# Time mix of a Perceiver block on one Trainium2 core: exponents from one difference, projections by feature chunk, gate product before the division

## Chip, cores and metric

The kernel runs on one core of one Trainium2 chip. The metric is device time in microseconds of one execution of the whole program, as the median of several runs. The kernel before takes 1672.26 us in the median of 3 runs (1671.02 to 1672.91).

## The reference, cut to the part concerned

The program is a two-layer Perceiver-like model on 8 sequences of 64 tokens with 512 features, all in float32: windowed attention, full attention, a quantised feed-forward layer, cross attention over 1601 context tokens, then an RWKV block (time mix and channel mix), and a small last layer. The change is inside the RWKV block's time mix. `time_first`, `time_decay` and the mixes are vectors over the 512 features.

```python
xa = _ln(x, ln1_g, ln1_b)
xx = _shift(xa)                       # one token back, zero before the first
xk = xa * time_mix_k + xx * (1 - time_mix_k)      # the same for xv, xr
k = xk @ att_Wk.T;  v = xv @ att_Wv.T;  r = xr @ att_Wr.T
w = -jnp.exp(time_decay)
def step(carry, kv_t):
    aa, bb, pp = carry
    kk, vv = kv_t
    ww = time_first + kk
    p = jnp.maximum(pp, ww)
    e1 = jnp.exp(pp - p)
    e2 = jnp.exp(ww - p)
    out = (e1 * aa + e2 * vv) / (e1 * bb + e2)
    ww2 = pp + w
    p2 = jnp.maximum(ww2, kk)
    e1b = jnp.exp(ww2 - p2)
    e2b = jnp.exp(kk - p2)
    return ((e1b * aa + e2b * vv, e1b * bb + e2b, p2), out)
rwkv = jax.nn.sigmoid(r) * out_of_all_steps
x = x + rwkv @ att_Wo.T
```

## The kernel before, in words

**Layout.** 512 tokens are 4 tiles of 128 (NT = 4), 512 features are 4 chunks of 128 (KC = 4). The time mix works with features on partitions: each chunk is a tile of 128 partitions by 512 tokens (8 sequences of 64), or by 520 where each sequence has one padding column for the past (`padded`). Everything is in SBUF; the weights `awk`, `awv`, `awr`, `awo` are loaded long before. PSUM has 8 banks of 128x512.

**Order.** There is no scheduler: each engine's instruction list is written out in its block function and runs in that order, and semaphores tie the lists together. In `time_mix`:

- PE turns the normalised input (`Turned.tensor`, L1487), ScalarE takes it out with gain and shift (L1493), GpSimd forms the difference to the past token (L1501), VectorE makes the mixes xk, xv, xr, a chunk at a time (L1508).
- PE then does the projections k, v and r (L1545 to L1553), each with all four chunks of its mix at hand, bank by bank: the outer loop goes over output chunks o, the inner one (in `linear_to_features`, L136) over input chunks c. k goes to banks 4 to 7, v to 0 to 3, r to 4 to 7. ScalarE copies k to `kp` (L1568), a chunk as soon as its bank is done.
- `exponents(o)` on VectorE: the running maximum `top` by a scan (L1620), the output's maximum `p_now` (L1626), the exponents of the present token in the output (p2, L1628) and of the past in the state (p3, L1629). GpSimd makes the other two, p1 (L1588) and p4 (L1589). `p_now` is double buffered, so VectorE waits for GpSimd two chunks behind.
- ScalarE takes the exponential of the four tiles in place (L1573), then copies v's chunk (L1575); after all four chunks it makes the sigmoid of r (L1578).
- GpSimd multiplies by v (L1594, L1595), for all four chunks; VectorE's `sums(o)` (L1635 to L1643) does the scans for denominator and numerator, products, sums, the reciprocal (L1641) and the product with it (L1643). GpSimd multiplies the result by the gate (L1599), queued behind its eight products.
- PE does the output projection when all four chunks of `gate` are ready (L1555), token tile by token tile (L128 in `linear_to_tokens`). VectorE adds each tile to the residual (L1651) and normalises it for the next block (L91, L92, L97), with two small GpSimd instructions in between (L110, L112).

The next block, `channel_mix`, starts when all of this is done, and only then issues the transfer of its second weight.

## Time and profile before

| | |
|---|---|
| median of 3 runs | 1672.26 us (1671.02 to 1672.91) |
| the profiled execution | 1670.92 us |
| its span in the trace | 1669.1 us |
| mean granted TensorE clock | 0.916 |
| busy in the span: PE, VectorE, ScalarE, GpSimd | 1452.6, 775.1, 466.5, 558.5 us |
| the time mix, from the first mix on VectorE to the last normalised tile | 1406.8 to 1504.6 us |

The span is the time from the first to the last instruction of the profiled execution; 1.8 us of that execution lie around it. Engines are PE (TensorE's matmuls), PEld (its weight loads), DVE (VectorE), ACT (ScalarE), POOL (GpSimd) and SP. A float32 matmul appears as two records, so a projection of 16 matmuls has 32. `<-` behind a bracketed number names what ended the idle time before the instruction. The shares of busy time over the whole span describe mostly the cross attention; for the time mix one has to read its own 98 us.

### The profile page before, as it was taken

The numbers are of one execution on the slowest core, as the hardware profiler recorded it, in microseconds if no ns is written. First come the engines' busy times: TensorE is split into PE (matmuls) and PEld (weight loads), VectorE is DVE, ScalarE is ACT, GpSimd is POOL, SyncE is SP. The second block draws the span as 40 slices with busy tenths as digits, with TensorE's granted clock in tenths as the row PEclk, the third lists the DMA queues.
The fourth block names the chain that finished last, engine by engine and source line by source line (L and its number), as shares of the span: only waits on it lengthen the run. The fifth ranks groups of instructions, "written<-read, shape, count | busy, mean of one in ns | idle before, by whom it ended". The sixth has DMA issues, their size and how long they took to land. (4 is left out here: it accounts for less than half of the span.)

```text
span 1669.1 us, 26535 instructions
## 1 busy us (share of the span) xinstructions
PE 1452.6 (87%) x11120; PEld 1061.9 (64%) x11120; DVE 775.1 (46%) x1333; ACT 466.5 (28%) x772; POOL 558.5 (33%) x315
## 2 busy tenths in 40 slices
PE   7778976567998999999999999999998896836796
PEld 3556765233544778888788888888886673315573
DVE  2454279989525342332323323222332316978913
ACT  0323201031112214243243433324243431303302
POOL 6101057656324043132122223132143224617701
PEclk9778965788998999999999999999999997967997
DMA  5300030010101411011011111111012116003000
GB/s 236 151 1 1 0 139 1 0 70 0 76 0 57 151 56 57 30 53 54 31 53 52 45 43 47 42 45 57 31 61 62 44 38 255 0 0 120 1 0 26
DMA packets 50101, 91.29 MB, mean 55 GB/s; under 512 B 28600, under 2 KB 41664, under 8 KB 46912
## 3 DMA queue, kind: packets, MB, share of 16 engines
q1 hardware_dynamic: 49984, 89.60, 15.2%
q8 instruction: 90, 1.47, 0.4%
q14 instruction: 27, 0.22, 0.0%
HBM read 79.89 MB, written 9.70 MB: 54 GB/s over the span
## 5 line engine op out<-in xcount | busy, mean ns | idle before, releaser
L1082 POOL TENSOR_TENSOR ctx_hi<-ctx_raw,one 128x1536 fp32r<-128x1536 f32 (+1 forms) x36 | 103.0, 2860 | 598.7 <-DMA ctx_raw<-in_ctx 369.6
L1367 DVE TENSOR_SCALAR_CACHE_REDUCE E<-PS 128x384 f32<-128x384 f32 (+1 forms) x256 | 131.8, 571 | 177.1 <-PE PS L1155 176.6
L1264 ACT COPY ET<-PS 128x512 f32<-128x512 f32 (+1 forms) x224 | 129.8, 586 | 292.5 <-PE PS L1178 223.5
L1336 DVE TENSOR_TENSOR V<-PS,vbias 128x512 f32<-128x512 f32 (+1 forms) x104 | 71.8, 691 | 218.4 <-PE PS L1122 218.3
L1178 PE MATMUL PS<-ident,E 128*128 128x128 f32 (+1 forms) x832 | 124.7, 275 | 8.9 <-ACT ET L1264 8.8
L1085 POOL TENSOR_TENSOR ctx_raw_r<-ctx_raw,ctx_hi 128x1536 fp32r<-128x1536 f32 (+1 forms) x36 | 131.3, 3647 | 2.8
L1122 PE MATMUL PS<-wv_lo,ctx_hi 128*128 128x512 f32 (+1 forms) x416 | 128.0, 408 | 0.0
L1122 PE MATMUL PS<-ctx_raw_r,wk_hi 128*128 128x384 f32 (+1 forms) x512 | 127.3, 354 | 0.0
L1122 PE MATMUL PS<-ctx_hi,wk_hi 128*128 128x384 f32 (+1 forms) x512 | 120.7, 357 | 2.3 <-POOL ctx_raw_r L1085 2.3
L1271 ACT ACTIVATE E<-E,peak 128x1601 f32<-128x1601 f32 x64 | 103.5, 1623 | 68.1 <-DVE peak L1372 68.1
L1122 PE MATMUL PS<-wv_hi,ctx_hi 128*128 128x512 f32 (+1 forms) x416 | 120.6, 412 | 0.8 <-issue 0.8
L1178 PEld LDWEIGHTS PS<-ident,E 128*128 128x128 f32 (+1 forms) x832 | 99.8, 140 | 28.6 <-ACT ET L1264 11.9
L1122 PE MATMUL PS<-ctx_hi,wk_lo 128*128 128x384 f32 (+1 forms) x512 | 113.8, 344 | 0.0
L1122 PE MATMUL PS<-wv_hi,ctx_raw_r 128*128 128x512 f32 (+1 forms) x416 | 113.6, 394 | 0.0
L1122 PEld LDWEIGHTS PS<-ctx_raw_r,wk_hi 128*128 128x128 f32 x512 | 90.1, 189 | 13.0 <-issue 11.0
L1122 PEld LDWEIGHTS PS<-ctx_hi,wk_hi 128*128 128x128 f32 x512 | 88.2, 189 | 13.4 <-issue 7.2
L1246 ACT ACTIVATE K<-PS,kbias 128x384 f32<-128x384 f32 x92 | 53.6, 582 | 147.5 <-PE PS L1122 147.5
L1122 PEld LDWEIGHTS PS<-ctx_hi,wk_lo 128*128 128x128 f32 x512 | 92.7, 188 | 2.0
L1122 PEld LDWEIGHTS PS<-wv_hi,ctx_hi 128*128 128x128 f32 (+1 forms) x416 | 71.4, 185 | 34.6 <-issue 20.5
L1122 PEld LDWEIGHTS PS<-wv_hi,ctx_raw_r 128*128 128x128 f32 (+1 forms) x416 | 76.4, 184 | 20.1
L1122 PEld LDWEIGHTS PS<-wv_lo,ctx_hi 128*128 128x128 f32 (+1 forms) x416 | 72.6, 185 | 20.5 <-issue 5.0
L1357 DVE TENSOR_TENSOR PS<-PS,corr 128x384 f32<-128x384 f32 x16 | 9.1, 567 | 121.3 <-PE PS L1155 107.2
(283 smaller groups left out, 2417.1 us busy)
## 6 DMA issues: line engine op xcount, KB each, us to landing
ctx_raw<-in_ctx SPq DMA_DIRECT2D x27, 768.0 KB, 4.5
ctx_raw<-in_ctx_first SPq DMA_DIRECT2D x9, 900.0 KB, 4.6
rel_scr<-rel_out SPq DMA_DIRECT2D x8, 640.0 KB, 3.7
fwk<-in_fwk SPq DMA_DIRECT2D x1, 4096.0 KB, 25.5
fwv<-in_fwv SPq DMA_DIRECT2D x1, 4096.0 KB, 12.5
corr<-rel_scr SPq DMA_DIRECT2D x64, 48.0 KB
p_scr<-E SPq DMA_DIRECT2D x16, 192.0 KB, 2.3
near<-p_scr SPq DMA_DIRECT2D x64, 48.0 KB
```

The lines of the kernel that those rows point to most:

```text
L1082: nc.gpsimd.tensor_tensor(ctx_hi[r][:, :, 0:n], ctx_raw[r][:, :, 0:n], one[:].unsqueeze(1).broadcast_to([P, KC, n]), ALU.mult).then_inc(S[ ...
L1085: nc.gpsimd.tensor_tensor(ctx_lo[r][:, :, 0:n], ctx_raw[r][:, :, 0:n], ctx_hi[r][:, :, 0:n].bitcast(F32), ALU.subtract).then_inc(S["split_ ...
L1122: last = nc.tensor.matmul(*products[k], start=(k == 0), stop=(k == 2 * half - 1))
L1178: last = nc.tensor.transpose(dst[0:n, r * P:(r + 1) * P], src(4 * o + r), s.ident[:])
L1246: nc.scalar.activation(K[c][:, j, 0:n], bank(4 + NUMBER[unit] % 2)[:, 0:n], ACT.Identity, bias=kbias[:, j:j + 1]).then_inc(S["k_out_act"], 1)
L1264: nc.scalar.copy(ET[0:n, j % ET_RING, :], src[0:n, :]).then_inc(S["et_out"], 1)
L1271: nc.scalar.activation(E[:, p, :], E[:, p, :], ACT.Exp, scale=scale, bias=peak[:, p:p + 1], accum_out=total[:, p:p + 1]).then_inc(S["exped ...
L1336: v.tensor_tensor(V[0:rows, at % V_RING, :], bank(4 + NUMBER[unit] % 2)[0:rows, :], vbias[0:rows, :], ALU.add).then_inc(S["v_out"], 1)
L1357: v.tensor_tensor(first, first, corr[:, 4 * o:4 * o + 4, :], ALU.add).then_inc(S["corrected"], 1)
L1367: v.tensor_scalar(E[:, p, k0:k0 + n], bank(r)[:, 0:n], 1.0, None, ALU.mult, ALU.max, accum_out=tops[:, p, c:c + 1]).then_inc(S["s_out"], 1)
```

## The change

1. **Exponents.** VectorE computes one tile per chunk, `step_of_k` = k minus the running maximum of the past. ScalarE makes the negatives of the four exponents from it with Relu, with a sign as scale and a column (exp(decay), its negative, first, its negative) as bias, then the four exponentials with scale -1. The separate exponents of VectorE and GpSimd, `p_now` and their semaphores go away. The four Relu of a chunk stand before its four Exp, and each Exp waits for its Relu.
2. **Projections.** k, v and r loop over input chunks outside and output chunks inside, and wait for one chunk of the mix at a time; the four banks of a projection finish in the last pass. r waits for all of k's copies.
3. **Gate.** GpSimd multiplies the numerator by the gate as soon as the numerator is summed, while VectorE takes the reciprocal; VectorE multiplies by the reciprocal afterwards, in `divide(o)`, which stands after `sums(o + 1)`.
4. **Output projection.** It also loops over chunks outside and token tiles inside, and waits for one chunk of `gate` at a time.

```diff
--- before.py
+++ after.py
@@ -1524,16 +1524,16 @@
     p3, p4 = padded("pow_past"), padded("pow_now")
     over_xn = Region(nc, s.xn_at)
     p1, p2 = over_xn.tensor("pow_out_past", [P, KC, B, SQ]), over_xn.tensor("pow_out_now", [P, KC, B, SQ])
-    wneg, p_now = m.tensor("wneg", [P, KC]), m.tensor("p_now", [P, 2, B, SQ])
+    wneg, wpos, nfirst = (m.tensor(n, [P, KC]) for n in ("wneg", "wpos", "nfirst"))
+    den = m.tensor("den", [P, 2, B, SQ])
     assert m.at <= s.fwk_at, m.at - s.fwk_at
 
     sum_v, sum_1 = kp, fade
-    num, out_now = diff, xa
-    den = p_now
+    step_of_k, num, out_now = diff, diff, xa
 
     tr = Turned(nc, sem, s, "b9_", vec, "ln1_g", "ln1_b")
-    names = ("mixed k_ps v_ps r_ps k_in v_in gate_in pads dve_step decay_exp top_done a_dve a_pool "
-             "exps num_pool out_done gated y_ps x_done").split()
+    names = ("mixed k_ps v_ps r_ps k_in v_in gate_in pads dve_step decay_exp biases top_done rectified "
+             "exps num_pool num_done num_gated gated y_ps x_done").split()
     S = {n: sem("b9_" + n) for n in names}
     bank = s.bank
     row = lambda ap: ap.rearrange("p b q -> p (b q)")
@@ -1543,34 +1543,47 @@
         def _(pe):
             tr.tensor(pe, nm)
             for i, (x, wn, done) in enumerate(((xk, "awk", "k_ps"), (xv, "awv", "v_ps"), (xr, "awr", "r_ps"))):
-                pe.wait_ge(S["mixed"], KC * (i + 1))
                 pe.wait_ge(s.loaded[wn], 16)
-                for o in range(KC):
-
-                    pe.wait_ge(tr.ready, KC)
-                    if i == 2:
-                        pe.wait_ge(S["k_in"], o + 1)
-                    linear_to_features(nc, bank(4 * ((i + 1) % 2) + o), w[wn], o, x[:].rearrange("p c b q -> p c (b q)")).then_inc(S[done], 1)
+                pe.wait_ge(tr.ready, KC)
+                if i == 2:
+                    pe.wait_ge(S["k_in"], KC)
+                for c in range(KC):
+                    pe.wait_ge(S["mixed"], KC * i + c + 1)
+                    for o in range(KC):
+                        last = nc.tensor.matmul(bank(4 * ((i + 1) % 2) + o), w[wn][:, c, o * P:(o + 1) * P],
+                                                x[:, c].rearrange("p b q -> p (b q)"), start=(c == 0), stop=(c == KC - 1))
+                        if c == KC - 1:
+                            last.then_inc(S[done], 1)
             pe.wait_ge(s.loaded["awo"], 16)
-            pe.wait_ge(S["gated"], KC)
-            for t in range(NT):
-                pe.wait_ge(S["v_in"], KC)
-                linear_to_tokens(nc, bank(t), gate[:].rearrange("p c b q -> p c (b q)"), t, w["awo"], 0, D).then_inc(S["y_ps"], 1)
+            pe.wait_ge(S["v_in"], KC)
+            for c in range(KC):
+                pe.wait_ge(S["gated"], c + 1)
+                for t in range(NT):
+                    last = nc.tensor.matmul(bank(t), gate[:, c].rearrange("p b q -> p (b q)")[:, t * P:(t + 1) * P], w["awo"][:, c, :],
+                                            start=(c == 0), stop=(c == KC - 1))
+                    if c == KC - 1:
+                        last.then_inc(S["y_ps"], 1)
 
         @block.scalar
         def _(act):
             act.wait_ge(s.loaded["vecs"], 16)
-            nc.scalar.activation(wneg[:], vec("decay"), ACT.Exp).then_inc(S["decay_exp"], 1)
+            nc.scalar.activation(wpos[:], vec("decay"), ACT.Exp).then_inc(S["decay_exp"], 1)
             tr.scalar(act, xa)
             split = lambda b: b.rearrange("p (b q) -> p b q", b=B)
             for o in range(KC):
                 act.wait_ge(S["k_ps"], o + 1)
                 nc.scalar.copy(kp[:, o, :, 1:], split(bank(4 + o))).then_inc(S["k_in"], 1)
+            act.wait_ge(S["biases"], 1)
             for o in range(KC):
-                act.wait_ge(S["a_dve"], 2 * o + 2)
-                act.wait_ge(S["a_pool"], 2 * o + 2)
-                for x in (p3[:, o, :, 1:], p4[:, o, :, 1:], p1[:, o], p2[:, o]):
-                    nc.scalar.activation(x, x, ACT.Exp).then_inc(S["exps"], 1)
+                act.wait_ge(S["top_done"], 2 * o + 2)
+                col = lambda x: x[:, o:o + 1]
+                powers = ((p3[:, o, :, 1:], 1.0, col(wpos)), (p4[:, o, :, 1:], -1.0, col(wneg)),
+                          (p1[:, o], 1.0, col(vec("first"))), (p2[:, o], -1.0, col(nfirst)))
+                for x, sign, bias in powers:
+                    nc.scalar.activation(x, step_of_k[:, o], ACT.Relu, scale=sign, bias=bias).then_inc(S["rectified"], 1)
+                for k, (x, _, _) in enumerate(powers):
+                    act.wait_ge(S["rectified"], 4 * o + k + 1)
+                    nc.scalar.activation(x, x, ACT.Exp, scale=-1.0).then_inc(S["exps"], 1)
                 act.wait_ge(S["v_ps"], o + 1)
                 nc.scalar.copy(vp[:, o, :, 1:], split(bank(o))).then_inc(S["v_in"], 1)
             for o in range(KC):
@@ -1583,10 +1596,6 @@
             for x, v in ((kp, PAST), (vp, 0.0), (p3, 0.0), (p4, 0.0)):
                 nc.gpsimd.memset(x[:, :, :, 0:1], v).then_inc(S["pads"], 1)
             tr.pool(pool, xa, diff)
-            for o in range(KC):
-                pool.wait_ge(S["top_done"], 2 * o + 2)
-                nc.gpsimd.tensor_tensor(p1[:, o], top[:, o, :, 0:SQ], p_now[:, o % 2], ALU.subtract).then_inc(S["a_pool"], 1)
-                nc.gpsimd.tensor_tensor(p4[:, o, :, 1:], kp[:, o, :, 1:], top[:, o, :, 1:], ALU.subtract).then_inc(S["a_pool"], 1)
             for o in range(KC):
 
                 pool.wait_ge(S["exps"], 4 * o + 4)
@@ -1595,8 +1604,8 @@
                 nc.gpsimd.tensor_tensor(out_now[:, o, :, 1:], p2[:, o], vp[:, o, :, 1:], ALU.mult).then_inc(S["num_pool"], 1)
             for o in range(KC):
                 pool.wait_ge(S["gate_in"], o + 1)
-                pool.wait_ge(S["out_done"], o + 1)
-                nc.gpsimd.tensor_tensor(gate[:, o], num[:, o], gate[:, o], ALU.mult).then_inc(S["gated"], 1)
+                pool.wait_ge(S["num_done"], o + 1)
+                nc.gpsimd.tensor_tensor(gate[:, o], num[:, o], gate[:, o], ALU.mult).then_inc(S["num_gated"], 1)
             for t in range(NT):
                 after.pool(pool, t)
 
@@ -1606,7 +1615,8 @@
             v = nc.vector
             dve.wait_ge(s.loaded["vecs"], 16)
             dve.wait_ge(S["decay_exp"], 1)
-            ch.link(v.tensor_scalar(wneg[:], wneg[:], -1.0, None, ALU.mult))
+            ch.link(v.tensor_scalar(wneg[:], wpos[:], -1.0, None, ALU.mult))
+            v.tensor_scalar(nfirst[:], vec("first"), -1.0, None, ALU.mult).then_inc(S["biases"], 1)
             for o in range(KC):
                 ch.add(v.tensor_copy(row(fade[:, o]), wneg[:, o:o + 1].broadcast_to([P, B * PADDED])))
             ch.sync()
@@ -1619,33 +1629,33 @@
                 dve.wait_ge(S["k_in"], o + 1)
                 v.tensor_tensor_scan(row(top[:, o]), row(fade[:, o]), row(kp[:, o]), PAST, ALU.add, ALU.max).then_inc(S["top_done"], 1)
                 dve.wait_ge(S["top_done"], 2 * o + 1)
-                if o >= 2:
-                    dve.wait_ge(S["a_pool"], 2 * o - 2)
-                first, past, now = vec("first")[:, o:o + 1], top[:, o, :, 0:SQ], top[:, o, :, 1:]
-                k = kp[:, o, :, 1:]
-                v.scalar_tensor_tensor(p_now[:, o % 2], k, first, past, ALU.add, ALU.max).then_inc(S["top_done"], 1)
-                dve.wait_ge(S["top_done"], 2 * o + 2)
-                v.scalar_tensor_tensor(p2[:, o], k, first, p_now[:, o % 2], ALU.add, ALU.subtract).then_inc(S["a_dve"], 1)
-                v.scalar_tensor_tensor(p3[:, o, :, 1:], past, wneg[:, o:o + 1], now, ALU.add, ALU.subtract).then_inc(S["a_dve"], 1)
+                v.tensor_tensor(step_of_k[:, o], kp[:, o, :, 1:], top[:, o, :, 0:SQ], ALU.subtract).then_inc(S["top_done"], 1)
 
             def sums(o):
 
                 dve.wait_ge(S["exps"], 4 * o + 4)
-                dve.wait_ge(S["a_pool"], 2 * (2 + o % 2) + 2)
                 ch.link(v.tensor_tensor_scan(row(sum_1[:, o]), row(p3[:, o]), row(p4[:, o]), 0.0, ALU.mult, ALU.add))
                 ch.add(v.tensor_tensor(den[:, o % 2], p1[:, o], sum_1[:, o, :, 0:SQ], ALU.mult))
                 dve.wait_ge(S["num_pool"], 2 * o + 2)
                 ch.link(v.tensor_tensor_scan(row(sum_v[:, o]), row(p3[:, o]), row(top[:, o]), 0.0, ALU.mult, ALU.add))
                 ch.add(v.tensor_tensor(num[:, o], p1[:, o], sum_v[:, o, :, 0:SQ], ALU.mult))
                 ch.link(v.tensor_tensor(den[:, o % 2], den[:, o % 2], p2[:, o], ALU.add))
+                v.tensor_tensor(num[:, o], num[:, o], out_now[:, o, :, 1:], ALU.add).then_inc(S["num_done"], 1)
                 ch.add(v.reciprocal(den[:, o % 2], den[:, o % 2]))
-                ch.link(v.tensor_tensor(num[:, o], num[:, o], out_now[:, o, :, 1:], ALU.add))
-                v.tensor_tensor(num[:, o], num[:, o], den[:, o % 2], ALU.mult).then_inc(S["out_done"], 1)
+
+            def divide(o):
+
+                ch.sync()
+                dve.wait_ge(S["num_gated"], o + 1)
+                v.tensor_tensor(gate[:, o], gate[:, o], den[:, o % 2], ALU.mult).then_inc(S["gated"], 1)
 
             for o in range(KC):
                 exponents(o)
             for o in range(KC):
                 sums(o)
+                if o >= 1:
+                    divide(o - 1)
+            divide(KC - 1)
             for t in range(NT):
                 dve.wait_ge(S["y_ps"], t + 1)
                 v.tensor_tensor(s.x0[:, t, :], s.x0[:, t, :], bank(t), ALU.add).then_inc(S["x_done"], 1)
```

## Rows read from the trace of the kernel before

**Rows 1.** The page, part 4: chain that ended last, shares of the span.

```profile
PE 1%; DVE 0%; ACT 0%; issue 0%; DVEq 0%
```

**Rows 2.** Table of stretches: microseconds, busy per engine (instructions), granted clock, DMA share, GB/s.

```profile
1400.00:1417.00 17.00, 8.83 (x25) 5.64 (x26) 13.55 (x22) 3.31 (x5) 6.48 (x12) 0.56 0.18 77
1417.00:1440.00 23.00, 23.00 (x55) 10.17 (x54) 21.98 (x18) 10.72 (x20) 12.40 (x9) 1.00 0.00 1
1440.00:1484.00 44.00, 14.84 (x35) 6.27 (x33) 42.65 (x32) 5.97 (x10) 19.10 (x12) 0.72 0.00 0
1530.00:1580.00 50.00, 38.59 (x150) 28.62 (x149) 50.00 (x38) 19.41 (x36) 43.44 (x28) 0.97 0.00 0
```

**Rows 3.** Timeline of VectorE, exponents: start, duration, line, operation, [idle <-releaser].

```profile
1417.80 1.24 DVE L1620 TENSOR_TENSOR_SCAN top<-fade,kp 128x520 f32<-128x520 f32 x1 [0.74 <-ACT kp L1568]
...
1421.55 1.76 DVE L1629 SCALAR_TENSOR_TENSOR pow_past<-top,wneg 128x512 f32<-128x512 f32 x1
1423.23 1.23 DVE L1620 TENSOR_TENSOR_SCAN top<-fade,kp 128x520 f32<-128x520 f32 x1
```

**Rows 4.** Timeline of VectorE, sums of chunks 0 to 2.

```profile
1439.53 2.33 DVE L1635 TENSOR_TENSOR_SCAN fade<-pow_past,pow_now 128x520 f32<-128x520 f32 x1
...
1453.44 1.23 DVE L1635 TENSOR_TENSOR_SCAN fade<-pow_past,pow_now 128x520 f32<-128x520 f32 x1
1454.71 1.57 DVE L1636 TENSOR_TENSOR p_now<-pow_out_past,fade 128x512 f32<-128x512 f32 x1
...
1458.79 3.35 DVE L1641 RECIPROCAL p_now<-p_now 128x512 f32<-128x512 f32 x1
...
1462.73 0.69 DVE L1643 TENSOR_TENSOR diff<-diff,p_now 128x512 f32<-128x512 f32 x1
1463.33 1.23 DVE L1635 TENSOR_TENSOR_SCAN fade<-pow_past,pow_now 128x520 f32<-128x520 f32 x1
```

**Rows 5.** Timeline of PE: k, v and output projections.

```profile
1411.81 15.56 PE L136 MATMUL PS<-xk,awk 128*128 128x512 f32 x32 [4.60 <-DVE xk L1508]
1427.21 13.90 PE L136 MATMUL PS<-xv,awv 128*128 128x512 f32 x32
...
1484.71 16.64 PE L128 MATMUL PS<-awo,gate 128*128 128x512 f32 x32 [29.87 <-issue]
```

**Rows 6.** Timeline of ScalarE: exponentials, table load; the last stage's Identity and Relu.

```profile
1428.94 0.62 ACT L1573 ACTIVATE pow_out_past<-pow_out_past 128x512 f32<-128x512 f32 x1
1429.46 0.62 ACT L1573 ACTIVATE pow_out_now<-pow_out_now 128x512 f32<-128x512 f32 x1
...
1442.32 1.28 ACT L1578 ACT_TABLE_LOAD   x1
...
1651.62 0.69 ACT L1853 ACTIVATE unit<-PS,kan 128x512 f32<-128x512 f32 x1 [6.35 <-PE PS L136]
1652.34 5.75 ACT L1858 ACTIVATE inner<-unit,kan 128x512 f32<-128x512 f32 x8
```

**Rows 7.** Timeline of GpSimd: products beside VectorE, beside a reciprocal, and alone.

```profile
1440.72 2.11 POOL L1595 TENSOR_TENSOR xa<-pow_out_now,vp 128x512 f32<-128x512 f32 x1
...
1451.07 1.18 POOL L1595 TENSOR_TENSOR xa<-pow_out_now,vp 128x512 f32<-128x512 f32 x1
...
1483.34 1.26 POOL L1599 TENSOR_TENSOR gate<-diff,gate 128x512 f32<-128x512 f32 x1 [7.83 <-DVE diff L1643]
```

**Rows 8.** Table of stretches, one microsecond.

```profile
1415.00:1416.00 1.00, 1.00 (x3) 0.38 (x2) 1.00 (x3) 0.00 (x0) 0.00 (x0) 1.00 0.00 0
```

**Rows 9.** Timeline of VectorE, residual and norm after the output projection.

```profile
1491.08 0.69 DVE L1651 TENSOR_TENSOR x<-x,PS 128x512 f32<-128x512 f32 x1 [7.88 <-PE PS L128]
...
1494.51 0.69 DVE L1651 TENSOR_TENSOR x<-x,PS 128x512 f32<-128x512 f32 x1 [0.25 <-PE PS L128]
...
1504.01 0.55 DVE L97 TENSOR_SCALAR XN<-x,mean_var,rstd 128x512 f32<-128x512 f32 x1 [1.00 <-POOL rstd L112]
```

**Rows 10.** Timeline of VectorE, the first mix.

```profile
1406.78 1.43 DVE L1508 SCALAR_TENSOR_TENSOR xk<-diff,vecs,xa 128x512 f32<-128x512 f32 x1 [1.08 <-POOL diff L1501]
```


## Prediction

> **What bounds the kernel now.** I read four kinds of view, in this order. First the chain that ended last: it lists one per cent of the span, all of it in the last stage [rows 1], so it says nothing of the time mix, and the stage has to be followed. Then the table of stretches: from 1417 to 1440 us VectorE is busy 21.98 of 23 us, from 1440 to 1484 us 42.65 of 44 us, while ScalarE has 10.72 and 5.97 [rows 2]. So VectorE alone sets the length of the time mix, from the first scan at 1417.80 to the last product. Then the timelines of the engines one by one. The exponents take 5.43 us a chunk (1417.80 to 1423.23) [rows 3], four times, to the first sum at 1439.53; the sums go from there to 1483.2, one chunk being 9.89 us when nearly undisturbed (1453.44 to 1463.33) and 13.91 us for the first (1439.53 to 1453.44), which runs beside GpSimd [rows 4]. Last, what follows: GpSimd's gate product 1.26 us [rows 7], then the output projection from 1484.71 [rows 5], whose first bank releases VectorE at 1491.08, and four rounds of residual and norm to 1504.56 [rows 9]. All blocks behind wait for that end, and move with it as a whole: their own DMAs are issued at the block's start, and the channel mix is bound by VectorE (50.00 of 50 us busy from 1530 to 1580) [rows 2]. So a microsecond taken from VectorE here is a microsecond of the kernel until another engine is late.
>
> One fact of sizes runs through all of it: a VectorE instruction with two SBUF inputs of 512 columns takes 0.69 us alone and 1.57 to 1.76 beside a GpSimd product [rows 3, 4]; a scan goes from 1.23 to 2.33. GpSimd's own go from 1.18 or 1.26 to 2.11 [rows 7]. I price a collision at 0.9 us of VectorE for each GpSimd product (1.57 less 0.69).
>
> **The change, part by part**, on the clock of the profiled execution.
>
> *Projections by chunk.* PE now starts when chunk 0 of xk is there, 1406.78 plus 1.43 [rows 10], so at 1408.3 in place of 1411.81 [rows 5]: 3.5 us earlier. But the four banks are now finished together at the end. A projection is 32 matmul records, 13.90 us at the high clock, 0.43 each [rows 5]. The k projection took 15.56, so 1.66 more: it had started at the low level. The granted clock is 1.00 (2.4 GHz) in the slice from 1415 [rows 8] and 0.56 on the mean of 1400 to 1417 [rows 2]; that is 0.50 (1.2 GHz) up to 1415, since (15 x 0.50 + 2 x 1.00) / 17 = 0.56. So it rose 3.2 us into the projection. The first k bank needs 26 records instead of 8: 26 x 0.429 + 1.66 = 12.8, so 1421.1, where it was about 1417.1. **The first scan goes from 1417.8 to about 1421.75: a loss of 3.9 us.** The last k bank, 6 records later, is ready at 1423.7, formerly 1427.4. The v projection follows at once; its first bank comes at 1423.65 + 26 x 0.429 = 1434.8 (before: 1427.21 and 8 records, 1430.7 [rows 5]), its last at 1437.4; r is done at 1451.1.
>
> *Exponents.* VectorE loses three scalar_tensor_tensor per chunk and gets one subtraction; GpSimd's two subtractions vanish, and with them the collisions. A chunk is a scan, 1.23 + 0.04, and a product at 0.69 with its step: 1.96 us instead of 5.43 [rows 3, 4]. Four chunks: 7.8 instead of 21.7, **a gain of 13.9 us**. They end at 1429.6.
>
> *ScalarE.* Per chunk four Relu and four Exp. Exp follows Exp every 0.52 us (1428.94, 1429.46) [rows 6]. A Relu with a bias column is not in the trace from SBUF; the nearest rows are 0.69 for an Identity with one column (a step of about 0.6) and 5.75/8 = 0.72 for a Relu with two columns [rows 6]. I take 0.62; the bounds are 0.52 and 0.72. A chunk is 4 x (0.62 + 0.52) = 4.56 us. Each Exp waits for the Relu four instructions ahead of it, which is long done: nothing. Chunk 0: 1424.2 to 1428.8. Then stands, in the same queue, the copy of v's bank 0, which comes only at 1434.8, and behind it is everything for chunks 1 to 3. This is **the new wait: ScalarE stands 6 us**, and so does GpSimd (it needs the v copy), and VectorE, which has done chunk 0's first scan and product by 1431.5. GpSimd's two products are 1435.5 to 1438.0 [rows 7], so VectorE idles 6.5 us, which it never did before. From there ScalarE delivers chunk 1 at 1439.9, 2 at 1445.0, 3 at 1450.1, its v copy at 1450.6, the table load of 1.28 us and the first sigmoid by 1452.5 [rows 6].
>
> The Trainium skill (ScalarE: Activation LUTs, Rules for kernel authors) says to use VectorE and not ScalarE for relu, which speaks against this step. The row here is the other way: one such exponent costs VectorE 1.76 us beside GpSimd and 0.69 without [rows 3, 4], and VectorE is the busy engine. Kept on VectorE, sixteen more at 0.65 a step would be 10.4 us, of which 6.5 fill the idle time found below: a gain of about 7 in place of 11.
>
> *Sums.* Per chunk the old 9.89 us contained one collision with the gate product (0.88) and the last product (0.60), which moves to divide [rows 4]: 8.4 us remain; 6.5 of them lie behind GpSimd's products. The reciprocal of 3.35 has one input, and GpSimd's products beside it ran at its undisturbed 1.18 (the one at 1451.07 [rows 7], while a reciprocal took 3.35 as ever [rows 4]), so what falls under it costs nothing. Chunk 0: 1438.0 to 1444.5, GpSimd's chunk 1 lies under its reciprocal. Chunk 1: 1444.5, 8.4 plus two products beside its scans (1.9) and a little of chunk 3's (0.4): 1455.2. Divide 0 needs the gated numerator, which GpSimd can make only after its eight products (1453.5) and the sigmoid: 1454.7, just in time. GpSimd's second gate product runs beside it (0.9 with the scan behind): 1456.5. Sum 2 to 1465.0, divide 1 to 1465.6, sum 3 to 1474.0, divide 2 to 1474.7, divide 3 to 1475.4. **Against GpSimd's last product, 1483.34 plus 1.26 [rows 7], that is 9.2 us, of which PE's start loses 0.1.**
>
> *Output projection.* Chunks 0 and 1 (8 records each) run at 1456.6 and 1465.7 in VectorE's shadow, at either clock level. At 1474.8 chunk 2 starts, and chunk 3 behind it. Token tile 0 is ready after 10 records: 4.3 us at the high clock, 8.6 at the low. The former start, after 29.87 us of idleness, took 16.64 for 32 records, 2.74 above 13.90, which is 5.5 us at the low level [rows 5]; the k projection showed 3.3. PE now worked until some 3 us before, so I take 3.3: 4.3 + 1.65 = 5.9, so 1480.7; bounds 4.3 and 8.6. Before, 8 records and 1491.08. **Gain so far 10.4 us.** The tail: a round was 3.43 us, because VectorE waited 0.25 for PE [rows 9]; the banks now come 0.86 us apart, so a round is its own 3.2 and four take 12.8 instead of 13.48: 0.65 more. End at 1493.5 instead of 1504.56: **gain 11.1 us.**
>
> The profiled execution took 1670.92 us, with a span of 1669.1; the median of the runs is 1672.26, some 1.3 above it. The same gain from the median: 1672.26 - 11.1 = 1661.2.
>
> **The rivals.**
> *Smaller gain.* All serial terms fall badly: the clock rises after 5.5 us both times (1.1 at k, which v's bank 0 and all behind it inherit, and 1.1 at the end, or 2.7 if it stays low), Relu steps at 0.72 (12 x 0.10, less 0.5 of slack: 0.7), two more collisions (1.8). Gain 11.1 - 4.7 = 6.4 to 8, about 1665. To this belongs the case that the change does not do what it says, the gate products not lying beside the reciprocals but each being waited for (1.26 us each, at most 5).
> *Larger gain.* The clock is high when the last burst starts (1.65), rises early in k (up to 1.65), and fewer products meet scans (1): 14 to 15, about 1657.5.
> *Table switches.* If Relu and Exp lay in different tables, each chunk would have two loads of 1.28; six of them fall behind v's bank 0, 7.7 us, less 0.5 of slack: gain 3.9, about 1668.4. Against it: the load at 1442.32 is the sigmoid's and the last of the run, and Relu and Identity run behind it without another [rows 6]; Relu with Exp is not in the trace. The Trainium skill (ScalarE: Activation LUTs, Table sets: the hidden batching unit) says that relu is in every set; no row of before shows it for the exp table.
> *Slower.* The chunk order keeps TensorE at the low level. It starts about a microsecond behind the transposes, with the clock at the low level, as the mean of 0.56 shows [rows 2]. If the clock did not rise, v's first bank, 58 records in, would come after 58 x 0.857 = 49.7 us in place of 26.5, at 1458, and everything behind it 23 us later: a loss of 12 us, 1684. The sign turns when the low stretch passes 3.3 + 22 us. Against it: the engine has no gap from 1408 to 1451, and the level rose 3.2 and 5.5 us into work in both places where it started low [rows 5, 8].
>
> **How the numbers follow.** Forecast, gain 8.5 to 13.5: 0.62. Larger: 0.12. Smaller, 5 to 8.5: 0.14. Table switches or something of that size, 3 to 5: 0.05, half of it beyond 0.2%. Nothing to be seen: 0.02. Slower: 0.05. A measurement of this kernel tells 0.2% (3.3 us) from no change; so faster 0.90, same 0.05, slower 0.05. The independent bounds (1.65 at k, 2.7 at the end, 1 for Relu, 2 for collisions, 1 for the median) reach some 4 to 5 us on either side: 1656.8 to 1666.8, which takes in the smaller and the larger gain and leaves out 0.15.
>
> **What the profile would show.** PE's first k record at 1408.3, but the first scan at 1421.7, later than now. Scan and subtraction back to back at 2.0 us a chunk, GpSimd silent there. On VectorE a gap of about 6.5 us inside the first sum, released by GpSimd, itself by ScalarE's v copy, itself by PE. No table load until the sigmoids. PE in bursts at 1457, 1466 and 1475. Rounds of 3.2 us in the tail. The prediction is wrong if v's first bank is late for another reason than its 58 records, if a Relu takes over a microsecond, if VectorE waits for the gate products in divide 2 or 3, or if a block behind this stage becomes longer.

## The result

The changed kernel takes 1662.03 us in the median of 4 runs (1661.28 to 1663.00), the kernel before 1672.51 beside it: 10.5 us less, ratio 0.9939 with a 95% interval of 0.9922 to 0.9956. The forecast was 1661.2. The profiled execution took 1662.66 us, span 1660.9.

The length of the stage tells more than the whole: from the first mix on VectorE to the end of the last normalised tile. It was 1406.78 to 1504.56, 97.78 us; it is 1409.56 to 1496.91, **87.35 us**. The 10.4 us lie there. What follows is 163.99 us (164.54 before); what precedes is the same code and began this stage between 1403.75 and 1411.35 in twelve profiles, so the 2.8 us by which it starts later are not counted as an effect of the change. Below, times with a plus are counted from the first mix.

Table of stretches (as [rows 2]), changed kernel:

```profile
1417.00:1440.00 23.00, 23.00 (x55) 10.10 (x54) 12.66 (x16) 10.58 (x19) 2.43 (x2) 1.00 0.00 1
1440.00:1475.00 35.00, 24.39 (x45) 10.13 (x44) 34.55 (x28) 15.26 (x27) 15.02 (x10) 0.80 0.00 0
```

VectorE, busy in 21.98 of the 23 us from 1417 to 1440 before, now works 12.66 of them, and is full (34.55 of 35) from 1440. Its timeline, to be held against [rows 3, 4, 9]:

```profile
1423.26 1.24 DVE L1630 TENSOR_TENSOR_SCAN top<-fade,kp 128x520 f32<-128x520 f32 x1 [3.42 <-ACT kp L1575]
1424.54 0.69 DVE L1632 TENSOR_TENSOR diff<-kp,top 128x512 f32<-128x512 f32 x1
1425.14 1.23 DVE L1630 TENSOR_TENSOR_SCAN top<-fade,kp 128x520 f32<-128x520 f32 x1
...
1439.49 1.24 DVE L1640 TENSOR_TENSOR_SCAN kp<-pow_past,top 128x520 f32<-128x520 f32 x1 [6.75 <-POOL xa L1604]
...
1442.10 1.78 DVE L1643 TENSOR_TENSOR diff<-diff,xa 128x512 f32<-128x512 f32 x1
...
1448.27 1.60 DVE L1638 TENSOR_TENSOR den<-pow_out_past,fade 128x512 f32<-128x512 f32 x1
1449.79 2.22 DVE L1640 TENSOR_TENSOR_SCAN kp<-pow_past,top 128x520 f32<-128x520 f32 x1
...
1452.65 1.77 DVE L1642 TENSOR_TENSOR den<-den,pow_out_now 128x512 f32<-128x512 f32 x1
1454.46 1.55 DVE L1643 TENSOR_TENSOR diff<-diff,xa 128x512 f32<-128x512 f32 x1
...
1459.31 0.69 DVE L1650 TENSOR_TENSOR gate<-gate,den 128x512 f32<-128x512 f32 x1
...
1477.44 1.29 DVE L1650 TENSOR_TENSOR gate<-gate,den 128x512 f32<-128x512 f32 x2
1484.48 0.69 DVE L1661 TENSOR_TENSOR x<-x,PS 128x512 f32<-128x512 f32 x1 [5.75 <-PE PS L1562]
...
1487.58 0.68 DVE L1661 TENSOR_TENSOR x<-x,PS 128x512 f32<-128x512 f32 x1
...
1496.36 0.55 DVE L97 TENSOR_SCALAR XN<-x,mean_var,rstd 128x512 f32<-128x512 f32 x1 [0.99 <-POOL rstd L112]
```

The first scan comes at +13.7 where it was +11.0; a chunk of exponents takes 1.88 us (1423.26 to 1425.14) instead of 5.43; then VectorE stands 6.75 us before the numerator of chunk 0. The chain of who waited for whom, and the instructions behind it on ScalarE and GpSimd (against [rows 6, 7]):

```profile
DVE kp L1640 <- POOL xa L1604: 6.8, 1, 6.8
ACT vp L1588 <- PE PS L1553: 6.0, 1, 6.0
```

```profile
1425.63 0.72 ACT L1583 ACTIVATE pow_past<-diff,wpos 128x512 f32<-128x512 f32 x1
1426.25 0.72 ACT L1583 ACTIVATE pow_now<-diff,wneg 128x512 f32<-128x512 f32 x1
...
1429.65 0.62 ACT L1586 ACTIVATE pow_out_now<-pow_out_now 128x512 f32<-128x512 f32 x1
1436.30 0.59 ACT L1588 COPY vp<-PS 128x512 f32<-128x512 f32 x1 [6.04 <-PE PS L1553]
...
1441.33 0.56 ACT L1588 COPY vp<-PS 128x512 f32<-128x512 f32 x1
...
1451.93 1.28 ACT L1591 ACT_TABLE_LOAD   x1
```

```profile
1437.03 1.28 POOL L1603 TENSOR_TENSOR top<-pow_now,vp 128x520 f32<-128x520 f32 x1 [23.70 <-ACT vp L1588]
1438.28 1.18 POOL L1604 TENSOR_TENSOR xa<-pow_out_now,vp 128x512 f32<-128x512 f32 x1
...
1447.04 2.27 POOL L1603 TENSOR_TENSOR top<-pow_now,vp 128x520 f32<-128x520 f32 x1 [2.13 <-ACT vp L1588]
...
1465.22 1.27 POOL L1608 TENSOR_TENSOR gate<-diff,gate 128x512 f32<-128x512 f32 x1 [6.87 <-DVE diff L1643]
```

ScalarE has chunk 0's exponentials at 1430.3, and stands 6.04 us for v's bank 0 with the work of three chunks behind it. GpSimd's products follow, then VectorE. No table load stands between Relu and Exp; the only one in the stage is the sigmoid's, at 1451.93. A Relu is followed by the next after 0.62 us. PE (against [rows 5]):

```profile
1411.14 13.97 PE L1553 MATMUL PS<-xk,awk 128*128 128x512 f32 x32 [1.14 <-DVE xk L1508]
1424.94 13.90 PE L1553 MATMUL PS<-xv,awv 128*128 128x512 f32 x32
...
1460.14 5.94 PE L1562 MATMUL PS<-awo,gate 128*128 128x512 f32 x8 [7.57 <-DVE gate L1650]
1469.12 6.58 PE L1562 MATMUL PS<-awo,gate 128*128 128x512 f32 x8 [3.04 <-DVE gate L1650]
1478.19 8.83 PE L1562 MATMUL PS<-awo,gate 128*128 128x512 f32 x16 [2.48 <-DVE gate L1650]
```

k's projection took 13.97 us, where it had taken 15.56: more on that below. The output projection comes in bursts of 8, 8 and 16 records.

### The profile page after: what moved, and what is told of

Its sections match the earlier page's. It is cut to its first block and busy times, and to the rows that moved or that the text cites. A ratio compares the mean times of both kernels' runs of the same rounds, so it can differ in the third digit from the quotient of the medians.

```text
span 1660.9 us, 26528 instructions
## 1 busy us (share of the span) xinstructions
PE 1456.5 (88%) x11120; PEld 1062.9 (64%) x11120; DVE 758.5 (46%) x1326; ACT 475.9 (29%) x788; POOL 544.1 (33%) x307
## 3 DMA queue, kind: packets, MB, share of 16 engines
q8 instruction: 90, 1.47, 0.4%
## 5 line engine op out<-in xcount | busy, mean ns | idle before, releaser
L1122 PEld LDWEIGHTS PS<-ctx_hi,wk_hi 128*128 128x128 f32 x512 | 88.2, 189 | 13.7 <-issue 7.2
L1155 PE MATMUL PS<-K,qT 32*64 32x384 f32 (+1 forms) x1024 | 60.1, 526 | 5.3 <-DVE E L1367 5.1
```

Source lines behind the costliest of these rows:

```text
L1122: last = nc.tensor.matmul(*products[k], start=(k == 0), stop=(k == 2 * half - 1))
L1155: last = nc.tensor.matmul(bank(r)[64 * gg:64 * gg + 64, 0:n], qT[rows, 2 * o + gg, b * SQ:(b + 1) * SQ], K[c][rows, 2 * o + gg, 0:n], star ...
```

## The experiments

To compare stages, the clock in the k projection has to be looked at each time: the first scan waits for its first bank, and that projection took 14.0, 15.4 to 15.7 or 16.8 us by the level at which PE's clock stood. The column "stage with k at 15.6" takes this out (stage, less what k took over 15.6, or plus what it took less). It doesn't take out the clock of the output projection; for that there is the column "output bank", the time from the start of that projection's last burst (of the whole projection where it runs token tile by token tile) to the first residual addition on VectorE. By it stages compare only to some 0.3 us, and the interleaved one has 1.7 us of its gain there. Ratios are to the kernel before, run beside each on the same chip, with 95% intervals.

| kernel | k took | stage | stage with k at 15.6 | output bank | ratio of time |
|---|---|---|---|---|---|
| before | 15.56 | 97.78 | 97.8 | 6.37 | 1 |
| changed | 13.97 | 87.35 | 89.0 | 6.29 | 0.9939 (0.9922 to 0.9956) |
| changed, again | 15.59 | 88.69 | 88.7 | 5.99 | 0.9951 (0.9932 to 0.9970) |
| exponents alone | 16.79 | 93.79 | 92.6 | 6.01 | 0.9984 (0.9970 to 0.9997) |
| gate and output alone | 16.80 | 94.29 | 93.1 | 6.24 | 0.9975 (0.9962 to 0.9987) |
| projections alone | 15.72 | 101.86 | 101.7 | 6.02 | 1.0007 (0.9990 to 1.0024) |
| changed, all bank by bank | 15.42 | 87.45 | 87.6 | 6.29 | 0.9949 (0.9931 to 0.9966) |
| the same, again | 15.69 | 87.75 | 87.7 | 6.30 | 0.9958 (0.9942 to 0.9973) |
| changed, v and r bank by bank | 15.64 | 84.21 | 84.2 | 6.29 | 0.9915 (0.9894 to 0.9937) |
| changed, v's copy moved back | 13.97 | 87.60 | 89.2 | 6.29 | 0.9934 (0.9916 to 0.9952) |
| changed, rectified on VectorE | 15.70 | 90.92 | 90.8 | 6.29 | 0.9947 (0.9932 to 0.9961) |
| interleaved | first bank 5.14 | 80.98 | 81 | 4.59 | 0.9896 (0.9881 to 0.9911) |

**The parts one by one.** The exponents alone, in the kernel before. Removed there as in the diff above are `p_now`, the exponents of VectorE and GpSimd; projections, sums and output stay.

```diff
...
-                v.scalar_tensor_tensor(p_now[:, o % 2], k, first, past, ALU.add, ALU.max) ...
...
-                v.scalar_tensor_tensor(p2[:, o], k, first, p_now[:, o % 2], ALU.add, ALU.subtract) ...
-                v.scalar_tensor_tensor(p3[:, o, :, 1:], past, wneg[:, o:o + 1], now, ALU.add, ALU.subtract) ...
+                v.tensor_tensor(step_of_k[:, o], kp[:, o, :, 1:], top[:, o, :, 0:SQ], ALU.subtract) ...
...
+                    nc.scalar.activation(x, step_of_k[:, o], ACT.Relu, scale=sign, bias=bias) ...
```

> The kernel before with the new exponents alone: one difference on VectorE, Relu and Exp on ScalarE; projections, sums, gate product and output projection as before. Theory A (most of the gain is VectorE's instructions and collisions taken out of the exponents): stage 90.6, a gain of 7.2 of 97.78, about 1665.3. Rival B (the exponents gain little by themselves since v and ScalarE take over the bound, the rest comes from the output): stage 93 to 96, 1668 or more.

Measured: 93.79, which lies in rival B's range, or 92.6 at one clock, a gain of 5.2 where 7.2 was expected; in whole runs 0.2%. That is neither theory's number, and both theories have a part in it.

```profile
1424.07 1.24 DVE L1623 TENSOR_TENSOR_SCAN top<-fade,kp 128x520 f32<-128x520 f32 x1 [1.39 <-ACT kp L1568]
...
1435.47 1.24 DVE L1630 TENSOR_TENSOR_SCAN fade<-pow_past,pow_now 128x520 f32<-128x520 f32 x1 [2.57 <-ACT pow_out_now L1579]
...
1451.29 2.32 DVE L1633 TENSOR_TENSOR_SCAN kp<-pow_past,top 128x520 f32<-128x520 f32 x1
1453.65 1.49 DVE L1634 TENSOR_TENSOR diff<-pow_out_past,kp 128x512 f32<-128x512 f32 x1
1455.06 1.75 DVE L1635 TENSOR_TENSOR den<-den,pow_out_now 128x512 f32<-128x512 f32 x1
```

The first two lines are the wait that the rival meant. Bank by bank, k's banks come 3.43 us apart (1424.07 and 1427.50 are two scans that each waited for one), and VectorE, which now needs 1.88 us a chunk, stands 1.39, 1.47 and 1.47 us for k's copies and 2.57 for ScalarE's exponentials. So of the 13.9 us that are taken from its exponents only 7.0 come off the time from the first scan to the first sum (14.76 us, before 21.73). From those 7.0 sum 1 takes back 2.1, by collisions, which is the shortfall from 7.2; the output projection's clock adds 0.35.

The last three lines are VectorE's timeline in sum 1: a scan of 2.32, a product of 1.49, a sum of 1.75, for 1.23, 0.69 and 0.69. The products of GpSimd, which stood beside the first sum alone before, now come chunk by chunk as ScalarE delivers, and meet sums 0 and 1 wherever a reciprocal does not happen to run: sum 0 takes 13.95 us from its first scan (with 1.08 of waiting) and sum 1 11.96, where sum 1 had been 9.89 [rows 4].

Gate product and output projection alone, in the kernel before:

```diff
...
+                v.tensor_tensor(num[:, o], num[:, o], out_now[:, o, :, 1:], ALU.add).then_inc(S["num_done"], 1)
                 ch.add(v.reciprocal(den[:, o % 2], den[:, o % 2]))
-                ch.link(v.tensor_tensor(num[:, o], num[:, o], out_now[:, o, :, 1:], ALU.add))
-                v.tensor_tensor(num[:, o], num[:, o], den[:, o % 2], ALU.mult).then_inc(S["out_done"], 1)
...
+                v.tensor_tensor(gate[:, o], gate[:, o], den[:, o % 2], ALU.mult).then_inc(S["gated"], 1)
```

> The kernel before with only the gate product beside the reciprocal, the division afterwards, and the output projection chunk by chunk; exponents and projections as before. The exponents alone gave 4.0 us of the stage of 97.78 (5.2 with the k projection at the same clock), less than the 7.2 expected, so these two parts must carry more than the 2 us that the prediction's sum left them. Theory A: three gate products no longer meet VectorE's sums (3 x 0.85 = 2.5), the first output bank comes 1 us earlier after the last gate, the tail's rounds are 3.2 instead of 3.43 (0.65): 4.2 us, stage 93.6, about 1666. Rival B (they only pay once VectorE is relieved): stage 96 to 97.8.

Measured: 94.29, at one clock 93.1, a gain of 4.7 for the 4.2 expected. The clean period shows where:

```profile
1465.58 0.69 DVE L1652 TENSOR_TENSOR gate<-gate,p_now 128x512 f32<-128x512 f32 x1
1466.19 1.24 DVE L1639 TENSOR_TENSOR_SCAN fade<-pow_past,pow_now 128x520 f32<-128x520 f32 x1
...
1474.65 0.69 DVE L1652 TENSOR_TENSOR gate<-gate,p_now 128x512 f32<-128x512 f32 x1
```

From one division to the next 9.07 us (1465.58 to 1474.65), where it was 9.89: GpSimd's gate product has gone from beside VectorE's first product of the next sum (1.57 us [rows 4], now 0.69) to beside the reciprocal. Three such chunks are 2.5 us, the tail's four rounds 1.05 (12.43 for 13.48). The gate product and the order of the output projection were not run apart, so the split of the 4.7 is read from this trace and not tested.

The projections alone, in the kernel before (the loops of the diff above and nothing else):

> The kernel before with only the projections looped by input chunk outside. Theory A (for k this order is a loss): VectorE is busy without a gap from its first scan on, and that comes with the first k bank, now the 26th record instead of the 8th, started 3.5 us earlier: 2.7 us later with the same clock at the start (4.3 if the rise comes late, 1.2 if at once). Stage 100.5 (99 to 102), slower than before by 2.7, about 1672.5 where before is 1669.8. Rival B (the earlier start is worth what the order costs): stage 97 to 98.

Measured: 101.86, a loss of 4, and in whole runs no difference that can be told (ratio 1.0007, 0.9990 to 1.0024). The sign is that of theory A. Its 2.7 was too small, though the clock of k was that of the kernel before (15.72 and 15.56): 18 more records at 0.43 are 7.7 us, and less the 3.5 of earlier start that is 4.2. 2.7 is what the changed kernel showed with k at 13.97.

```profile
1426.80 1.24 DVE L1623 TENSOR_TENSOR_SCAN top<-fade,kp 128x520 f32<-128x520 f32 x1 [5.16 <-ACT kp L1571]
```

The first scan is at +15.45 (first mix at 1411.35), 4.4 later than the +11.02 of [rows 3], and everything behind it moved with it, since VectorE has no gap after it: its last product comes 4.4 later too, and the output projection gives 0.35 back by its clock.

**The order of the projections in the changed kernel.** All of them bank by bank again:

```diff
+                pe.wait_ge(S["mixed"], KC * (i + 1))
...
-                for c in range(KC):
-                    pe.wait_ge(S["mixed"], KC * i + c + 1)
-                    for o in range(KC):
-                        last = nc.tensor.matmul(bank(4 * ((i + 1) % 2) + o), ...
...
+                for o in range(KC):
...
+                    linear_to_features(nc, bank(4 * ((i + 1) % 2) + o), w[wn], o, ...).then_inc(S[done], 1)
```

> The changed kernel with k, v and r projected bank by bank again, all chunks of the mix waited for, as before. Measure: the stage from the first mix on VectorE to the last normalised tile, 97.78 us before, 87.35 in the changed kernel. Theory A (the chunk order costs, because all four banks come last, and ScalarE's queue stands behind v's bank 0): the first k bank comes 2.7 us earlier, the last 5 later, v's bank 0 2.8 earlier; ScalarE takes chunk 0's exponents only after all four k copies, so VectorE resumes the first sum 1 us earlier: stage 86.3, about 1661. Rival B (the earlier start of the projections is what pays): stage 89 to 91, 1664 to 1666.

Measured: stage 87.45 with k at 15.42, where 86.3 was expected and 89 to 91 by the rival. Against the changed kernel's 87.35 that looks like a tie, but k had its slow start here: at one clock it is 87.6 against 89.0. Whether the clock explains the tie was then tried by running the pair again on one chip:

> The changed kernel again, beside the version with bank-by-bank projections on one chip. Theory A (the chunk order costs 1.5 us in the changed kernel at one and the same clock of the k projection; the changed kernel's own profile had k at 13.97 us, all others but one at 15.4 to 16.8, which hid it): with k at 15.6 the stage is 88.9, with k at 13.97 it is 87.35; the median of the runs lies 0 to 2 us above that of the bank-by-bank version. Rival B (the order gains): it lies over 1 us below.

> The changed kernel with k, v and r bank by bank, the same file as before, as the partner of the run beside it. Theory A: stage 87.2 to 87.6 with k at 15.4 to 15.6, median 0 to 2 us below the changed kernel. Rival B: median over 1 us above.

```profile
1410.00:1411.00 1.00, 0.00 (x0) 0.00 (x0) 1.00 (x2) 0.78 (x1) 1.00 (x2) 0.95 0.00 0
```

```profile
1412.00:1413.00 1.00, 1.00 (x2) 0.42 (x2) 1.00 (x2) 0.00 (x0) 0.10 (x1) 0.50 0.00 0
1413.00:1414.00 1.00, 1.00 (x3) 0.38 (x2) 1.00 (x3) 0.00 (x0) 0.00 (x0) 0.92 0.00 0
```

```profile
1409.90 15.59 PE L1553 MATMUL PS<-xk,awk 128*128 128x512 f32 x32 [1.14 <-DVE xk L1508]
```

These are stretches of the changed kernel's first profile (one line) and its second (two), and the second's k projection. In the first the granted clock rose (0.95 on the mean of the slice) in the pause between the transposes and k's first matmul, which came at 1411.14; in the second it stood at 0.50 until 1413, 3 us into the projection. The same kernel has its first scan at +13.70 and +15.31 by this, and 87.35 and 88.69 us of stage; 0.3 of the 1.6 came back in the output projection (6.29 and 5.99).

With k at 15.59 and 15.69 the chunk order costs 88.69 - 87.75 = 0.9 us of stage, where 1.5 was expected. The clock of the output projection doesn't enter if one compares VectorE's last product: it ends at +70.81 against +69.56 here, and at +69.17 against +69.27 in the first pair. Put to 15.6 for k in all four, the order costs 1.35 us in either pair. In whole runs (medians 1661.60 and 1661.95) nothing of this is seen: the changed kernel's is 0.35 lower, where 0 to 2 higher was expected, and the intervals of the ratios, 0.9932 to 0.9970 and 0.9942 to 0.9973, are wider than the effect.

**What the gap hangs on.** Only v and r bank by bank, k by chunk:

> The changed kernel with only v and r projected bank by bank, k still by chunk. Theory A (VectorE's gap of 6.75 us in the first sum comes only from v's bank 0 being in the 26th record and from ScalarE's queue behind its copy): v's bank 0 is ready 8 us earlier, the gap falls to under 0.5 us, ScalarE never stands; part of the gain comes back as collisions with GpSimd's products (2 us more); stage 82 (80.5 to 83.5), about 1657. Rival B (ScalarE with 24 instructions after the copy, or GpSimd behind it, is itself the bound): a gap of several us stays on VectorE at chunk 1 or 2, stage 85 to 87.

```profile
1432.94 1.60 DVE L1643 TENSOR_TENSOR den<-pow_out_past,fade 128x512 f32<-128x512 f32 x1
1435.62 1.24 DVE L1645 TENSOR_TENSOR_SCAN kp<-pow_past,top 128x520 f32<-128x520 f32 x1 [1.07 <-POOL xa L1609]
1436.89 1.72 DVE L1646 TENSOR_TENSOR diff<-pow_out_past,kp 128x512 f32<-128x512 f32 x1
1438.54 1.67 DVE L1647 TENSOR_TENSOR den<-den,pow_out_now 128x512 f32<-128x512 f32 x1
```

The gap on VectorE falls from 6.75 to 1.07 us, and the stage to 84.21: 4.5 under the changed kernel with the same clock (88.69), where 5.4 (87.35 to 82) were expected. The numerator's scan comes 4.7 us earlier than there: the gap is 5.7 shorter, and the product ahead of it took 1.60 for 0.69, since GpSimd now works beside it. From that scan to the last product both kernels take the same 39.2 us, so the collisions behind it (1.72 and 1.67 in the two lines, three more in sum 1) only stand in other places. Rival B falls: ScalarE doesn't stand between the exponentials, and VectorE has no gap at chunks 1 and 2.

This version also parts k from v. It differs from the one with all projections bank by bank in k alone, and its last product comes 3.5 us earlier (+66.03 against +69.56, k at 15.64 and 15.69). So the chunk order of v and r costs 4.8 us here and that of k gains 3.5: with all of k's banks there, VectorE does the four short chunks of exponents without the waits that the exponents alone had shown.

Whether ScalarE's standing costs anything by itself, with v's order left alone:

```diff
-                act.wait_ge(S["v_ps"], o + 1)
-                nc.scalar.copy(vp[:, o, :, 1:], split(bank(o))).then_inc(S["v_in"], 1)
+                for u in {0: (), 1: (0, 1), 2: (2,), 3: (3,)}[o]:
+                    act.wait_ge(S["v_ps"], u + 1)
+                    nc.scalar.copy(vp[:, u, :, 1:], split(bank(u))).then_inc(S["v_in"], 1)
```

> The changed kernel with the copy of v's bank 0 moved in ScalarE's list behind the exponentials of chunk 1, so that ScalarE doesn't stand 6 us before them; the order of the projections is unchanged. Theory A (the gap of 6.75 us on VectorE hangs on v's bank 0 alone; ScalarE's standing costs nothing more, since VectorE needs chunk 1 only 8 us later): the gap stays at 6.3 to 7, the stage at 86.5 to 87.5 with k at 13.97 us (up to 1.7 more with a slower k). Rival B (ScalarE's standing is what costs): chunk 1 to 3 come 5 us earlier and the stage falls to 83 or less.

```profile
1434.43 2.31 DVE L1641 TENSOR_TENSOR_SCAN kp<-pow_past,top 128x520 f32<-128x520 f32 x1 [6.76 <-POOL xa L1605]
```

The same gap, 6.76 us, and a stage of 87.60 against 87.35 at the same k. ScalarE is some 4 us ahead with chunks 2 and 3 (its last copy of v at +37.65 against +41.78) and nothing comes of it: theory A. GpSimd's products of chunks 1 and 2 now fall beside sum 0, whose reciprocal ends 2.8 us later (the scan above took 2.31 for 1.24), and sum 1 gets that back. The long wait on ScalarE was true and worth nothing; only its first link, v's bank 0, was on the path.

**The rectification on VectorE.**

```diff
...
+                for x, col, op in ((p3[:, o, :, 1:], wpos, ALU.max), (p4[:, o, :, 1:], wpos, ALU.min),
+                                   (p1[:, o], vec("first"), ALU.max), (p2[:, o], vec("first"), ALU.min)):
+                    v.tensor_scalar(x, step_of_k[:, o], col[:, o:o + 1], 0.0, ALU.add, op).then_inc(S["rectified"], 1)
```

> The changed kernel with the sixteen rectifications on VectorE, as one tensor_scalar each (add a column, then max or min with 0), ScalarE doing only the exponentials. Theory A (VectorE is the busy engine, its 6.75 us gap hides part): sixteen at about 0.5 us are 8 us, the first sum resumes 2.4 us later, and GpSimd's products, now earlier, meet more of VectorE's: stage 90 (89 to 92), about 1665. Rival B (the gap hides all and ScalarE, relieved of 2.5 us a chunk, gives back time): stage 86 to 87.5, no slower than the changed kernel.

```profile
1427.50 0.49 DVE L1632 TENSOR_SCALAR pow_past<-diff,wpos 128x512 f32<-128x512 f32 x1
1427.90 0.48 DVE L1632 TENSOR_SCALAR pow_now<-diff,wpos 128x512 f32<-128x512 f32 x1
...
1439.45 1.52 DVE L1632 TENSOR_SCALAR pow_out_now<-diff,vecs 128x512 f32<-128x512 f32 x1
1440.89 2.21 DVE L1637 TENSOR_TENSOR_SCAN fade<-pow_past,pow_now 128x520 f32<-128x520 f32 x1
```

Stage 90.92 with k at 15.70, 2.2 above the changed kernel at that clock, of which 0.3 is the output projection's; up to the last product it is 1.8. A rectification is 0.49 us with a step of 0.40, sixteen are 6.4 us, and the gap of 6.75 would hide them; but the gap was also what kept VectorE out of GpSimd's way. The last rectification took 1.52 for 0.48, the first scan of the sums 2.21, and the whole of sum 0 runs beside GpSimd: seven instructions lose 6.8 us together, where five lose 4.9 in the changed kernel. That is the 1.8. The medians show no loss (0.9947 to the changed kernel's 0.9951): in this profile the part behind the stage was 161.61 us instead of 163.6 to 164.5, for the most part because the first matmuls of the last stage ran at the high clock (8 records in 3.70 us against 6.12 in the changed kernel's). That belongs to no edit: of the two profiles of the version with all bank by bank, which are the same kernel, one has it and one has not (161.37 and 164.40 behind the stage, 3.70 and 6.18 for the 8 records). It is one more reason to compare stages.

**A version from the theory.** k and v alternate bank by bank, ScalarE takes a chunk's k copy, exponentials and v copy in turn, VectorE does a chunk's exponents just ahead of the sums of the chunk before:

```diff
...
+            for o in range(KC):
+                project(0, o)
+                project(1, o)
+            for o in range(KC):
+                project(2, o)
...
+            exponents(0)
+            exponents(1)
+            sums(0)
+            exponents(2)
+            sums(1)
+            exponents(3)
+            sums(2)
+            divide(0)
+            divide(1)
+            sums(3)
+            divide(2)
+            divide(3)
```

> A version from the theory: the changed kernel, but bank by bank with k and v alternating (k0 v0 k1 v1 ...), ScalarE taking k's chunk, its eight exponent instructions and v's chunk in turn, VectorE doing the exponents of a chunk just ahead of the sums of the one before, a third buffer for the denominator, the divisions of chunks 0 and 1 after sum 2. Theory A (VectorE is the bound from the moment that its first sum can be completed, so what counts is how early v's bank 0 and chunk 0's exponentials are there): sum 0 completes from 21 us after the first mix instead of 29.9, the last division at 62 instead of 69: stage 80.5 (79 to 82.5), about 1652 to 1654. Rival B (waits for k banks between sums, or collisions with GpSimd, eat it): no better than v and r bank by bank, 83 to 85.

VectorE, and the output projection's last burst on PE:

```profile
1433.06 1.24 DVE L1641 TENSOR_TENSOR_SCAN kp<-pow_past,top 128x520 f32<-128x520 f32 x1
...
1436.27 3.35 DVE L1645 RECIPROCAL den<-den 128x512 f32<-128x512 f32 x1
...
1460.64 3.33 DVE L1651 TENSOR_TENSOR gate<-gate,den 128x512 f32<-128x512 f32 x2 [0.69 <-POOL gate L1609]
```

```profile
1473.10 7.13 PE L1564 MATMUL PS<-awo,gate 128*128 128x512 f32 x16 [0.63 <-DVE gate L1651]
```

Stage 80.98, 1655.43 us, ratio 0.9896 (0.9881 to 0.9911): as expected in the stage (80.5), a little over it in time (1652 to 1654). It is faster than the changed kernel, and has the lowest median of all here, though its interval overlaps that of v and r bank by bank (0.9894 to 0.9937). Chunk 0's numerator starts at +23.9 (first mix at 1409.15) instead of +29.9; all of GpSimd's eight products but the first two lie beside reciprocals. What is lost is a wait of 5.66 us for k's chunk 1, ahead of the first sum, and at divisions 0 and 1, where VectorE waits 0.69 and then takes 3.33 us for two products of 0.69, beside three gate products. Of the 3.2 us by which its stage is under that of v and r bank by bank, 1.5 are there by the last product. The other 1.7 are PE's clock: the output projection comes in two bursts with 0.63 us between them, the second ran 16 records in 7.13 us where the changed kernel needed 8.83 after 2.48 us of idle time, and its first bank came after 4.59 us instead of 6.29.

## Why the prediction was right, and where it was not

- **PE's start and k's first bank.** Start at +1.5, measured +1.58. The first bank was put at +14.3 with k at 15.56; it came at +13.0, since the clock was up when k began. In the second profile, with k at 15.59, the first scan was at +15.3 (forecast +15.0). The term was 1.66 us for the low clock; it was 0.1 once and 1.7 once, and no run here shows what decides between the two. Its lower bound of 0 had been in the range.
- **Exponents.** 1.96 us a chunk forecast, 1.88 measured. Relu's step, taken as 0.62 between 0.52 and 0.72, is 0.62. ScalarE's chunk of 5.1 us with its copy is 5.03 (1436.30 to 1441.33).
- **The new wait.** 6.5 us forecast, 6.75 measured, with the chain as told: PE, ScalarE's v copy, GpSimd, VectorE. The weight given to ScalarE's queue was too much: it stood 6.04 us as forecast, and taking 4.5 of them away changed nothing.
- **Collisions were under-counted.** This is the term that failed in size; the mechanism was as told. Sum 0 was to run free from 1438.0 and ended a microsecond late (the 1.78 at 1442.10 beside a product of chunk 1). Sum 1 was 12.25 us (1447.06 to 1459.31) where 10.7 was forecast: four of its six instructions met GpSimd, at 2.22, 1.60, 1.77 and 1.55. The price of 0.9 us was nearly right: five slowed instructions lost 4.9 us. The number was wrong: two products beside sum 1 and a little of chunk 3's were counted, 2.3 us, and five products of GpSimd fell beside the two sums, one of chunk 1 ahead of the reciprocal and both of chunk 3. Together that is 2.6 us too little, of which some 0.6 came back, since the late sum 1 put GpSimd's second gate product under the reciprocal. (The 1.3 us allowed there for division 0 and that product would be 1.5 by the working's own 0.6 and 0.9.)
- **Output.** First bank 5.9 us after the last burst's start, measured 6.29 (1478.19 to 1484.48). The 3.3 us at the low clock were nearly right, it stood at 0.50 from 1478.4 to 1481.8; the working had left out some 0.2 us from a bank's last record to VectorE, which the kernel before has too (6.37 for 3.43 + 2.74). The tail's rounds were to be 3.2, and are 3.1: 12.43 us in place of 12.8.
- **The sum.** Gain in the stage 11.1 forecast, 10.43 measured. The clock gave 1.3 that was not counted, the collisions took 2.0, the output's 0.4 too much and the tail's 0.4 too little cancel. At the clock of the kernel before, the change is worth 97.8 - 88.7 = 9.1 us. So the forecast of the time was better than its parts, and that is luck: with k's start at the clock that the working assumed, the gain would have been 2 us under the 11.1. On another chip the pair gave 1668.75 and 1661.60, 7.2 us.
- **Which part pays.** Alone, the exponents give 5.2 us and gate with output 4.7. Together, that is the changed kernel with the projections bank by bank: 97.8 - 87.7 = 10.1, so they add. The working named for the output only 1.2 and for the tail 0.65; the gate product's way out of the sums (three times 0.82) had gone into the sums' 8.4 us, as the 0.88 taken off a chunk, and was not added up as the gate's part, so nearly all looks like the exponents' gain. The chunk order of the projections is a loss, 3.9 us alone and 1.35 in the changed kernel. The step on the first bank had said so for k; but it had k and v as one: once the exponents are short, k's chunk order gains 3.5 us, and that of v and r costs 4.8.
- **The rivals.** No table load appeared; the Trainium skill's statement that relu is in every set (ScalarE: Activation LUTs, Table sets: the hidden batching unit) is what the trace shows for the exp table. On VectorE the rectification cost 2.2 us of stage, less than the 4 worked out for it: one tensor_scalar steps at 0.40 us and not 0.65, so the gap would have hidden all sixteen, and what is left are collisions that the working had not in it. The Trainium skill's rule to use VectorE for relu (ScalarE: Activation LUTs, Rules for kernel authors) is by these 2.2 us the slower choice here, where VectorE is the busy engine. The clock did not stay low.

## What to carry to other kernels

When an engine is relieved, ask in which bank or chunk of the engine before it the new first need lies: a loop order that finishes all outputs together puts the first of them last, which cost 4.8 us for v, whose first bank was waited for, and gained 3.5 for k, all of whose banks were soon wanted. A long wait on a side engine is not a cost until moving it moves the end; here 6 us of ScalarE standing were free, and the 6.75 of VectorE behind the same bank were not. Two engines that slow each other down have to be placed in time, here GpSimd's products under VectorE's reciprocals; take the collisions instruction by instruction, not by a mean.

## What the runs showed of the hardware

- VectorE beside GpSimd: products and sums with two SBUF inputs 1.49 to 1.78 us for 0.69, scans 2.2 to 2.3 for 1.23; but the changed kernel's scan at 1447.06 took 1.17 while GpSimd's product beside it took 2.27, so which of the two pays differs; a tensor_scalar, with one tensor input, 1.52 for 0.48 once, which was not expected. The reciprocal took 3.34 to 3.35 in every case, with and without GpSimd beside it.
- The clock of PE can rise in a pause: in one profile of the changed kernel it went from 0.50 to 1.00 at about 1410, between the transposes and the k projection. One and the same kernel has the first projection at 13.97 or 15.59 us by that, and another, in its two profiles, the first matmuls of the last stage at 3.70 or 6.18. That is 1.6 and 2.5 us, as much as the smaller of the edits here.
